# Cross-attention on one core: the third head group's last probability sum behind the fourth group's first maximum, and the hand-on of the largest weight moved into the third batch

## Chip, cores, metric

The kernel runs on one core of a Trainium2 chip. The metric is the time on the device in microseconds, of one execution. All times in this text are microseconds unless they are marked ns. The engines are TensorE (PE, and PEld for its weight loads), VectorE (DVE), ScalarE (ACT), GpSimd (POOL) and SyncE (SP, which issues most DMA transfers).

## What is computed

One block of a perceiver: x (8 batches of 128 rows of 512) attends to a context (8 batches of 2048 rows), then to itself with weights and activations quantised to 8 bits, then goes through a mixture of 8 experts. The change touches the first third and one number that the second needs, the largest absolute weight.

```python
def cross_attention(query, context, Wq, Wk, Wv, Wo):      # 16 heads of 32
    Q, K, V = query @ Wq.T, context @ Wk.T, context @ Wv.T
    scores = einsum('bqhd,bkhd->bhqk', Q, K) / sqrt(32)
    attn = softmax(scores, axis=-1)
    return einsum('bhqk,bkhd->bqhd', attn, V).reshape(B, 128, 512) @ Wo.T

def fake_quant(x):                                        # per tensor, 8 bits
    scale = maximum(max(abs(x)) / 127, 1e-8)
    return round(clip(x / scale, -128, 127)) * scale

x = x + cross_attention(layernorm(x), ctx_1024, ...)
x = x + self_attention_quantised(layernorm(x), fake_quant(in_w), fake_quant(out_w), ...)
x = x + experts(layernorm(x), ...)
```

## The kernel before

Everything around the change is `cross_attention`. It runs over 8 batches (b = 0 to 7) and in each over 4 head groups of 4 heads (g = 0 to 3); the order on each engine is written out by hand, in one `body(b, last)` for each engine, and the engines meet by semaphores. About 136 us go by per batch.

For each group TensorE first makes the scores of 128 queries and 2048 keys in four pieces of 512 keys (`scores_for_max`, L900), each for four heads at once into `sc`, all four banks of it. VectorE reads each piece and takes the maximum per row (`maximum`, L656); TensorE may write the next piece only when the maximum has read the last (semaphore `m_read`). Between the pieces TensorE works on projections of keys or values for later groups (L861, L875), so that it need not stand still. Then the maxima go through a diagonal matrix (`maxima_to_diag`, L660, L664) and one matmul into a row of the stacked queries `qs` (L915), and TensorE makes the scores a second time, transposed and less the maximum (`scores_transposed`, L935), in 8 units of 256 keys. For that the keys have to be stacked in `ks` (high and low halves, moved by 12 DMA transfers of SP's queue for each group, `stack_k`, L298), and the queries in `qs` (12 transfers for each batch, L288). ScalarE takes the exponential of each unit into `probs` (L489), which has room for four units. TensorE multiplies each with the values (`times_v`, L952).

The denominators of the softmax are the sums over keys. VectorE adds units 0, 1, 4, 5, 6 into `acc_v` in four instructions (`add_probs(b, g, part)`, part 0 at L675, parts 1 to 3 at L678); GpSimd adds units 2, 3 and 7 into `acc_g` (L383, L388), then `acc_v` to it (L391, which waits for all four of VectorE's parts by `sum_v`) and folds it (L393). TensorE turns that into denominators (`denominators`, L972) after the four score pieces of the group that follows.

VectorE also makes the low halves of the next group's keys (`split_k`, L616), which the key stack and a bank of `proj` wait for, and in the third and fourth group the low halves of the next batch's context (`split_ctx`, L610). In the fourth group's case the last part of the sums already stands behind the first maximum of the next batch; in the other three groups it stands before the next group's first maximum. In batch 0 VectorE also takes the maximum over pieces of the weights (`largest_weight`, L810).

The pieces of the weights come by GpSimd's queue (`load_weight`, L347): four in each group of batch 0. When VectorE has seen all 16 (batch 1, group 1), it sets `wmax_ready`. GpSimd hands the two partial maxima on between batch 1 and batch 2: out to DRAM in `wmax` (L418), a wait until they have landed, and back to all partitions in `wq_all`, which lies in `xn2` (L420). Behind that it loads the first two weight pieces again, for the quantisation in the last batch.

Of the kernel before, what the change touches and what calls it, by code (L numbers as in the profile page):

```python
# [14 lines left out]
P = 128  # L15
B, T, D = 8, 128, 512
# [89 lines left out]
def cross_attention(nc, x, ctxT, wqT, wkT, wvT, woT, wiT, qoT, in_b, weights_q, wmax, wscale, wide_stage, stage_in, shared, x1, x1_stats, ident, ident16, ones, ones16):  # L106
# [4 lines left out]
    with ExitStack() as c:  # L111
# [154 lines left out]
        with nc.Block() as block:  # L266
# [71 lines left out]
            def _(gp):  # L338
                gp.memset(ks[QK:P, :, :], 1.0).then_inc(rows_set, 1)

                def load_weight(n, round_trip):
# [4 lines left out]
                        gp.wait_ge(wq_seen, WPIECES)  # L346
                    gp.dma_start(wq_f[:, n % 2, :], weight_piece(n)).then_inc(wq_in[n % 2], 16)  # L347

                def quantise_weight(n):
                    which = n // (3 * EC)  # L350
                    gp.wait_ge(wq_in[n % 2], 16 * (WPIECES // 2 + n // 2 + 1))
                    gp.tensor_scalar(wq_f[:, n % 2, :], wq_f[:, n % 2, :], wq_inv[:, which:which + 1], ROUND,
                                     ALU.mult, ALU.add).then_inc(wq_int, 1)
                    gp.wait_ge(wq_int, 2 * n + 1)
                    if n >= 2:
                        gp.wait_ge(wq_out[n % 2], 16 * (n // 2))
                    gp.tensor_scalar(wq_i[:, n % 2, :], wq_f[:, n % 2, :], -ROUND, 1.0, ALU.add, ALU.mult).then_inc(wq_int, 1)
                    gp.wait_ge(wq_int, 2 * n + 2)
                    gp.dma_start(weights_q[:, n // EC, n % EC, :], wq_i[:, n % 2, :]).then_inc(wq_out[n % 2], 16)
                    if n + 2 < WPIECES:  # L360
                        load_weight(n + 2, 1)
# [9 lines left out]
                def body(b, last):  # L371
                    for g in range(G):
                        e = 32 * b + UNITS * g
                        if first_batch(b) and g:
                            load_weight(4 * g, 0)
                            load_weight(4 * g + 1, 0)

                        at = 16 * b + 4 * g
                        if not (last and g == 3):
                            gp.wait_ge(e_ready, e + 4)  # L380
                            if not (isinstance(b, int) and b == 0 and g == 0):
                                gp.wait_ge(group_done, 4 * b + g)
                            gp.tensor_tensor(acc_g[:, :], probs[:, 2, :], probs[:, 3, :], ALU.add).then_inc(sum_g, 1)  # L383
                            if first_batch(b):
                                load_weight(4 * g + 2, 0)
                            gp.wait_ge(e_ready, e + 8)
                            gp.wait_ge(sum_g, at + 1)
                            gp.tensor_tensor(acc_g[:, :], acc_g[:, :], probs[:, 3, :], ALU.add).then_inc(sum_g, 1)  # L388
                            gp.wait_ge(sum_v, at + 4)
                            gp.wait_ge(sum_g, at + 2)  # L390
                            gp.tensor_tensor(acc_g[:, :], acc_g[:, :], acc_v[:, :], ALU.add).then_inc(sum_g, 1)  # L391
                            gp.wait_ge(sum_g, at + 3)
                            gp.tensor_tensor(acc_g[:, 0:512], acc_g[:, 0:512], acc_g[:, 512:1024], ALU.add).then_inc(sum_g, 1)  # L393
                        if first_batch(b):
                            load_weight(4 * g + 3, 0)
                        if last:
                            for n in range(*((0, 6), (6, 11), (11, WPIECES), (WPIECES, WPIECES))[g]):
                                if n == 2 * EC:
                                    gp.wait_ge(rows_scaled, 1)
                                    normalise(0)  # L400
                                    normalise(1)
                                quantise_weight(n)
                            if g == 2:
                                normalise(2)
                                normalise(3)
# [7 lines left out]
                load_weight(1, 0)  # L413
                body(0, False)

                body(1, False)
                gp.wait_ge(wmax_ready, 1)
                gp.dma_start(wmax[:, :], wq_part[:, :]).then_inc(wmax_moved, 16)  # L418
                gp.wait_ge(wmax_moved, 16)
                gp.dma_start(wq_all[:, :, :], wmax.rearrange("(a p) w -> a p w", a=1).to_broadcast([P, P, 2])).then_inc(wmax_moved, 16)  # L420
                load_weight(0, 1)
                load_weight(1, 1)
                for b in range(2, B - 1):
                    body(b, False)
                gp.wait_ge(wq_scaled, 1)
                body(B - 1, True)
# [172 lines left out]
            def _(dve):  # L599
# [120 lines left out]
                def body(b, last, steps):  # L720

                    first = first_batch(b)
                    for g in range(G):
                        for kb in range(KB):
                            maximum(b, g, kb)
                            if g == 0 and kb == 0 and not first:
                                add_probs(b - 1, 3, 3)
                            if first and g == 1 and kb:
                                row_stats(range((1, 4, 6)[kb - 1], (4, 6, 8)[kb - 1]), steps)
                            if first and g == 2 and kb == 0:  # L730
# [50 lines left out]
                        for part in range(4):  # L781
                            if ahead and part == 1:
                                split_k(nb, ng, 1)
                                if g == 2 and not last:
                                    split_ctx(b + 1, 2)
                            if g < 3 or not last and part < 3:
                                add_probs(b, g, part)
                            if ahead and part > 1:
                                split_k(nb, ng, part)
# [1686 lines left out]
```

## Time and profile before

| | us |
|---|---|
| median of 3 runs | 1725.7 |
| lowest and highest | 1724.34, 1726.32 |
| span of the profiled execution | 1727.4 |

The page gives no time for the profiled execution but its span, so that is what a sum is made against.

| engine | busy us | share of the span |
|---|---|---|
| PE | 1628.6 | 94% |
| DVE | 1171.3 | 68% |
| ACT | 767.5 | 44% |
| POOL | 471.1 | 27% |

The cross-attention fills the span up to about 1126 us, the quantised self-attention to about 1265, and the experts the rest. TensorE is close to full throughout, so small holes in its timeline count and what other engines do beside it does not, as long as it doesn't wait for them. In a timeline an idle time before an instruction stands in brackets, with the engine and line that ended it.

### The profile page before, as it was taken

How to read it: one execution, taken by the hardware profiler on the slowest of the kernel's cores; microseconds unless marked ns; L12 is line 12 of the kernel's file. 1: busy time of each engine (PE TensorE's matmuls, PEld its weight loads, DVE VectorE, ACT ScalarE, POOL GpSimd, SP SyncE). 2: the span in 40 equal slices, each digit the busy share in tenths (PEclk: the TensorE clock that was granted, in tenths of full speed). 3: DMA queues.
4: the chain of work that ended last, by engine and by line, in shares of the span. 5: the costliest groups of instructions: out<-in, count | busy, mean ns of one | idle time of the engine just before them, and what ended most of it. 6: DMA issues, size and time to landing. Idle time of an engine off the chain costs nothing. (4 is left out here: it accounts for less than half of the span.)

```text
span 1727.4 us, 39816 instructions
## 1 busy us (share of the span) xinstructions
PE 1628.6 (94%) x17264; PEld 1111.9 (64%) x17264; DVE 1171.3 (68%) x1400; ACT 767.5 (44%) x973; POOL 471.1 (27%) x412
## 2 busy tenths in 40 slices
PE   6999999999999999999999999896669999999998
PEld 4666666666666766666666666674447777777775
DVE  5678567457657757656766757557787767666766
ACT  5354336344444444435434533545445444344441
POOL 2323322232123123212222237632025411101133
PEclk9999999999999999999999999997879999999999
DMA  6544243334234233242233225460048655555544
GB/s 246 124 110 111 60 116 87 62 88 122 47 87 110 60 87 87 52 111 72 67 82 95 74 59 138 121 232 2 2 138 263 214 188 180 196 174 186 180 129 121
DMA packets 102151, 202.04 MB, mean 117 GB/s; under 512 B 25739, under 2 KB 25739, under 8 KB 101850
## 3 DMA queue, kind: packets, MB, share of 16 engines
q1 hardware_dynamic: 91258, 169.49, 34.1%
q0 software_dynamic: 10720, 30.02, 6.3%
q8 instruction: 137, 2.24, 0.6%
q14 instruction: 36, 0.29, 0.1%
HBM read 127.36 MB, written 18.90 MB: 85 GB/s over the span
## 5 line engine op out<-in xcount | busy, mean ns | idle before, releaser
L656 DVE TENSOR_REDUCE mx<-sc 128x4 f32<-128x2048 f32 x128 | 293.2, 2290 | 67.0 <-PE sc L900 66.4
L861 PE MATMUL proj<-w_hi,ctx 128*128 128x256 f16 x2048 | 273.7, 278 | 12.8 <-ACT ctx L441 12.6
L489 ACT ACTIVATE stage_w<-sc 128x1024 f32<-128x1024 f32 x256 | 248.2, 1024 | 70.8 <-PE sc L935 70.2
L875 PE MATMUL proj<-ctx,w_hi 128*128 128x512 f16 x1024 | 253.6, 380 | 0.0
L861 PEld LDWEIGHTS proj<-w_hi,ctx 128*128 128x128 f16 x2048 | 193.0, 99 | 64.6 <-issue 40.4
L452 ACT ACTIVATE stage_w<-proj 128x512 f32<-128x512 f32 x128 | 76.4, 597 | 340.8 <-PE proj L861 340.8
L383 POOL TENSOR_TENSOR acc_g<-stage_w 128x1024 f32<-128x1024 f32 x31 | 74.0, 2389 | 477.0 <-ACT stage_w L489 476.9
L678 DVE TENSOR_TENSOR acc_v<-acc_v,stage_w 128x1024 f32<-128x1024 f32 x93 | 131.9, 1418 | 87.1 <-ACT stage_w L489 84.3
L616 DVE SCALAR_TENSOR_TENSOR k_lo<-proj,k_hi 128x512 f16<-128x512 f32 x128 | 88.0, 687 | 118.6 <-ACT k_hi L461 117.7
L1166 DVE SCALAR_TENSOR_TENSOR w_lo<-stage_w,w_hi 128x2048 f16<-128x2048 f32 x64 | 144.8, 2293 | 34.2 <-ACT w_hi L1160 34.2
L875 PEld LDWEIGHTS proj<-ctx,w_hi 128*128 128x128 f16 x1024 | 90.1, 98 | 116.5 <-issue 25.1
L861 PE MATMUL proj<-w_lo,ctx 128*128 128x256 f16 x1024 | 157.9, 278 | 1.2 <-DVE w_lo L604 1.2
L1994 ACT ACTIVATE hf<-ph 128x321 f32<-128x321 f32 x128 | 56.3, 440 | 213.4 <-PE ph L2277 195.8
L2293 PE MATMUL po<-h_hi,w_hi 128*128 128x321 f16 x496 | 149.2, 301 | 0.3 <-issue 0.3
L2293 PE MATMUL po<-h_lo,w_hi 128*128 128x321 f16 x496 | 149.3, 301 | 0.0
L2293 PE MATMUL po<-h_hi,w_lo 128*128 128x321 f16 x496 | 149.2, 301 | 0.0
L935 PEld LDWEIGHTS sc<-qs,stage_w 97*128 97x128 f16 x2048 | 126.7, 99 | 32.8 <-DMA stage_w<-k_hi 5.0
L935 PE MATMUL sc<-qs,stage_w 97*128 97x128 f16 x2048 | 138.4, 221 | 5.3 <-DMA stage_w<-k_hi 3.5
L952 PE MATMUL po<-stage_w 128*32 128x128 f32 x4096 | 139.4, 277 | 0.0
L875 PE MATMUL proj<-ctx,w_lo 128*128 128x512 f16 x512 | 131.8, 380 | 0.0
L461 ACT ACTIVATE k_hi<-proj 128x512 f16<-128x512 f32 x128 | 76.5, 597 | 108.9 <-PE proj L875 104.1
L388 POOL TENSOR_TENSOR acc_g<-acc_g,stage_w 128x1024 f32<-128x1024 f32 x31 | 80.7, 2604 | 152.0 <-ACT stage_w L489 152.0
(354 smaller groups left out, 2488.8 us busy)
## 6 DMA issues: line engine op xcount, KB each, us to landing
stage_w<-in_w SPq DMA_DIRECT2D x64, 1024.0 KB, 5.9
ctx_stage<-in_ctxT SPq DMA_DIRECT2D x64, 512.0 KB, 4.6
stage_w<-k_hi SPq DMA_DIRECT2D x256, 128.0 KB, 2.4
stage_w<-k_lo SPq DMA_DIRECT2D x128, 128.0 KB, 2.4
wq_f<-in_wiT POOLq DMA_DIRECT2D x24, 256.0 KB, 4.4
xg<-xbuf POOLq DMA_DIRECT2D x28, 176.0 KB, 4.4
obuf<-o_sb POOLq DMA_DIRECT2D x28, 176.0 KB, 3.5
xbuf<-final SPq DMA_DIRECT2D x17, 256.0 KB
```

The costliest lines, as they stand in the source:

```text
L388: gp.tensor_tensor(acc_g[:, :], acc_g[:, :], probs[:, 3, :], ALU.add).then_inc(sum_g, 1)
L461: act.activation(k_hi[:, 512 * kb:512 * kb + 512], proj[where % 2][:, :], ACT.Copy, scale=1.0 / WSCALE).then_inc(proj_act, 1)
L489: act.activation(probs[:, u % 4, :], unit_scores(u), ACT.Exp, scale=1.0 / sqrt(HD)).then_inc(e_ready, 1)
L616: dve.scalar_tensor_tensor(k_lo[part], proj[where % 2][:, :], 1.0 / WSCALE, k_hi[part], ALU.mult, ALU.subtract).then_inc(k_low, 1)
L656: dve.tensor_reduce(mx[:, :, kb], sc[:, :, :], AX.X, ALU.max).then_inc(m_read, 1)
L678: dve.tensor_tensor(acc_v[:, :], acc_v[:, :], probs[:, (0, 0, 1, 2)[part], :], ALU.add).then_inc(sum_v, 1)
L861: last = pe.matmul(out, x_part[:, kb, e, col:col + P], w_part[:, 2, e, wv], start=term == 0 and e == 0, stop=term == 2 and e == EC - 1)
L875: last = pe.matmul(proj[at % 2][:, :], w_part[:, 1, e, P * (g % G):P * (g % G) + P], x_part[:, kb, e, :], start=term == 0 and e == 0, stop ...
L935: last = pe.matmul(sc[:, 2 * (u % 2) + i, P * j:P * j + P], ks[0:QKM, j, P * ck:P * ck + P], qs[0:QKM, 4 * g + j, :], start=True, stop=True)
L952: last = pe.matmul(po[HD * j:HD * j + HD, 0:T], v_sb[:, g // 2, ck, at:at + HD], probs[:, u % 4, 512 * i + P * j:512 * i + P * j + P], sta ...
L1166: dve.scalar_tensor_tensor(w_lo[:, s % NSPLIT], stage[:, s], WSCALE, w_hi[:, s % NSPLIT], ALU.mult, ALU.subtract).then_inc(stage_lo, 1)
L2293: last = pe.matmul(po[i][:, 0:CAP], w_part[:, s % NSPLIT, f, P * i:P * i + P], h_part[:, at, :], start=q == 0 and f == 0 and n == 0, stop= ...
```

## The change

VectorE: part 3 of the sums of the third group (g = 2) is no longer issued at the end of that group but behind the first maximum of the fourth (g = 3), in all eight batches.

GpSimd: the hand-on of the two partial maxima (a wait, a DMA, a wait until it has landed, a DMA) moves from between batch 1 and batch 2 into the first group of batch 2, between GpSimd's first and second add. The two weight loads that stood behind it move to the same place in the second group of batch 2.

```diff
+                def hand_on_largest():
+                    gp.wait_ge(wmax_ready, 1)
+                    gp.dma_start(wmax[:, :], wq_part[:, :]).then_inc(wmax_moved, 16)
+                    gp.wait_ge(wmax_moved, 16)
+                    gp.dma_start(wq_all[:, :, :], wmax.rearrange("(a p) w -> a p w", a=1).to_broadcast([P, P, 2])).then_inc(wmax_moved, 16)
...
                             if first_batch(b):
                                 load_weight(4 * g + 2, 0)
+                            if b == 2 and g == 0:
+                                hand_on_largest()
+                            if b == 2 and g == 1:
+                                load_weight(0, 1)
+                                load_weight(1, 1)
                             gp.wait_ge(e_ready, e + 8)
...
-                body(1, False)
-                gp.wait_ge(wmax_ready, 1)
-                gp.dma_start(wmax[:, :], wq_part[:, :]).then_inc(wmax_moved, 16)
-                gp.wait_ge(wmax_moved, 16)
-                gp.dma_start(wq_all[:, :, :], wmax.rearrange("(a p) w -> a p w", a=1).to_broadcast([P, P, 2])).then_inc(wmax_moved, 16)
-                load_weight(0, 1)
-                load_weight(1, 1)
-                for b in range(2, B - 1):
+                for b in range(1, B - 1):
                     body(b, False)
...
                             if g == 0 and kb == 0 and not first:
                                 add_probs(b - 1, 3, 3)
+                            if g == 3 and kb == 0:
+                                add_probs(b, 2, 3)
...
-                            if g < 3 or not last and part < 3:
+                            if g < 2 or part < 3 and not (last and g == 3):
                                 add_probs(b, g, part)
```

What the change moves on VectorE, at the step from the third to the fourth group of batch 1. The add into `acc_v` is part 3 of the sums, `k_lo` is the key split, `mx<-sc` a maximum. Before:

```order
L616 SCALAR_TENSOR_TENSOR k_lo<-proj0,k_hi 128x512
L610 TENSOR_TENSOR ctx<-ctx_stage,ctx 128x1024
L678 TENSOR_TENSOR acc_v<-acc_v,stage_w 128x1024
L616 SCALAR_TENSOR_TENSOR k_lo<-proj1,k_hi 128x512
L656 TENSOR_REDUCE mx<-sc 128x4 x4
L660 TENSOR_REDUCE nm<-mx 128x4
```

And now, in the changed kernel, whose lines are numbered a little higher:

```order
L620 SCALAR_TENSOR_TENSOR k_lo<-proj0,k_hi 128x512
L614 TENSOR_TENSOR ctx<-ctx_stage,ctx 128x1024
L620 SCALAR_TENSOR_TENSOR k_lo<-proj1,k_hi 128x512
L660 TENSOR_REDUCE mx<-sc 128x4
L682 TENSOR_TENSOR acc_v<-acc_v,stage_w 128x1024
L660 TENSOR_REDUCE mx<-sc 128x4 x3
```

The add went from ahead of the last key split to behind the first of the four maxima.

On GpSimd, from the end of batch 1 to the second group of batch 2. The adds into `acc_g` are the sums of the probabilities. Before:

```order
L393 TENSOR_TENSOR acc_g<-acc_g 128x512
L418 DMA wmax<-wq_part 128x2
L420 DMA xn2<-wmax 128x256
L347 DMA wq_f<-in_wiT 128x512 x2
L383 TENSOR_TENSOR acc_g<-stage_w 128x1024
L388 TENSOR_TENSOR acc_g<-acc_g,stage_w 128x1024
L391 TENSOR_TENSOR acc_g<-acc_g,acc_v 128x1024
```

And now:

```order
L404 TENSOR_TENSOR acc_g<-acc_g 128x512
L389 TENSOR_TENSOR acc_g<-stage_w 128x1024
L351 DMA wmax<-wq_part 128x2
L353 DMA xn2<-wmax 128x256
L399 TENSOR_TENSOR acc_g<-acc_g,stage_w 128x1024
L402 TENSOR_TENSOR acc_g<-acc_g,acc_v 128x1024
L404 TENSOR_TENSOR acc_g<-acc_g 128x512
L389 TENSOR_TENSOR acc_g<-stage_w 128x1024
L347 DMA wq_f<-in_wiT 128x512 x2
L399 TENSOR_TENSOR acc_g<-acc_g,stage_w 128x1024
```

Two of the four DMAs went behind the first add of batch 2, the other two behind the first add of its second group.

## Rows read from the trace of the kernel before

**Rows 1.** The page, busy time, share and instructions of each engine
```profile
PE 1628.6 (94%) x17264; PEld 1111.9 (64%) x17264; DVE 1171.3 (68%) x1400; ACT 767.5 (44%) x973; POOL 471.1 (27%) x412
```
**Rows 2.** Who waited for whom: total us, times, longest
```profile
PE sc L900 <- DVE mx L656: 18.2, 18, 2.9
```
**Rows 3.** Timeline (start, length), TensorE, group 3's score pieces, batches 2 and 1
```profile
418.23 0.40 PE L900 MATMUL sc<-k_hi,q_hi 32*128 32x512 f16 x4
...
423.27 0.40 PE L900 MATMUL sc<-k_hi,q_hi 32*128 32x512 f16 x4 [1.91 <-DVE mx L656]
...
426.32 0.40 PE L900 MATMUL sc<-k_hi,q_hi 32*128 32x512 f16 x4
...
280.74 0.40 PE L900 MATMUL sc<-k_hi,q_hi 32*128 32x512 f16 x4 [1.92 <-DVE mx L656]
...
285.46 0.40 PE L900 MATMUL sc<-k_hi,q_hi 32*128 32x512 f16 x4
```
**Rows 4.** Stretches: busy by engine, then granted clock, DMA share, GB/s
```profile
280.00:286.00 6.00, 5.26 (x34) 3.40 (x35) 2.98 (x3) 0.84 (x2) 1.48 (x2) 0.72 0.92 206
334.00:341.40 7.40, 7.26 (x25) 3.96 (x26) 1.92 (x2) 2.54 (x3) 0.00 (x0) 0.59 0.01 2
```
**Rows 5.** Timeline, VectorE, last add and first maximum, batch 2
```profile
416.93 3.39 DVE L678 TENSOR_TENSOR acc_v<-acc_v,stage_w 128x1024 f32<-128x1024 f32 x1
...
420.85 2.27 DVE L656 TENSOR_REDUCE mx<-sc 128x4 f32<-128x2048 f32 x1
```
**Rows 6.** Timeline, GpSimd and ScalarE, the same place
```profile
416.17 3.07 POOL L388 TENSOR_TENSOR acc_g<-acc_g,stage_w 128x1024 f32<-128x1024 f32 x1 [4.44 <-ACT stage_w L489]
...
417.33 0.60 ACT L461 ACTIVATE k_hi<-proj 128x512 f16<-128x512 f32 x1 [1.23 <-PE proj L875]
```
**Rows 7.** Timeline, TensorE and VectorE, first group of batch 3
```profile
457.78 0.39 PE L900 MATMUL sc<-k_hi,q_hi 32*128 32x512 f16 x4
...
460.95 0.40 PE L900 MATMUL sc<-k_hi,q_hi 32*128 32x512 f16 x4
...
457.38 1.22 DVE L678 TENSOR_TENSOR acc_v<-acc_v,stage_w 128x1024 f32<-128x1024 f32 x1
```
**Rows 8.** Timeline, TensorE, fourth group of batch 0
```profile
144.32 0.40 PE L900 MATMUL sc<-k_hi,q_hi 32*128 32x512 f16 x4 [2.95 <-DVE mx L656]
```
**Rows 9.** Timeline, TensorE and VectorE, fourth group of batch 7
```profile
1098.58 1.91 PE L92 MATMUL proj<-ctx_stage,wi_q 128*128 128x256 f16 x16 [1.62 <-issue]
...
1107.04 2.29 DVE L656 TENSOR_REDUCE mx<-sc 128x4 f32<-128x2048 f32 x1 [0.59 <-PE sc L900]
```
**Rows 10.** Timeline and DMA list (last: us to landing), hand-on and what follows
```profile
321.45 0.56 POOL L418 DMA_DIRECT2D wmax<-wq_part  x1
...
325.36 0.55 POOL L420 DMA_DIRECT2D xn<-wmax  x1 [3.36 <-DMA wmax<-wq_part]
...
wq_f<-in_wiT POOLq DMA_DIRECT2D x2, 256.0 KB, 7.2
...
334.14 1.89 PE L935 MATMUL sc<-qs,stage_w 97*128 97x128 f16 x16 [3.55 <-DMA stage_w<-k_hi]
...
335.82 5.74 PE L1021 MATMUL misc<-wo_sb,ot 128*128 128x512 f32 x8
...
343.12 1.06 PE L935 MATMUL sc<-qs,stage_w 97*128 97x128 f16 x16
...
472.18 3.65 PE L1021 MATMUL misc<-wo_sb,ot 128*128 128x512 f32 x8
```
**Rows 11.** Timeline, GpSimd, TensorE and SP's queue, the new places in batch 2
```profile
353.27 2.48 POOL L388 TENSOR_TENSOR acc_g<-acc_g,stage_w 128x1024 f32<-128x1024 f32 x1 [5.03 <-ACT stage_w L489]
...
377.22 2.37 POOL L383 TENSOR_TENSOR acc_g<-stage_w 128x1024 f32<-128x1024 f32 x1 [17.63 <-ACT stage_w L489]
...
367.66 0.43 PE L972 MATMUL po<-acc_g,ones 128*32 128x128 f32 x8
...
387.32 2.42 SPq L298 DMA_DIRECT2D stage_w<-k_hi  x4
```

## Prediction

> **What bounds the kernel now.** I read the page first, for the engine that fills the span: TensorE is busy for 94% of it, VectorE for 68%, so time can be won only where TensorE stands still or runs slowly [rows 1]. Next the list of who waited for whom, for TensorE inside the cross-attention: its reading of scores L900 waited 18.2 us in all, 18 times, for VectorE's maxima L656 [rows 2]. Then TensorE's timeline at those places. Three things are to be seen.
>
> First, the same wait stands at the same place in every batch but the last: between the first and the second score group of the fourth head group. The score groups of the third batch start at 418.23, 423.27 and 426.32 [rows 3]. The undisturbed distance is 426.32 - 423.27 = 3.05; the disturbed one is 5.04, so this place costs 1.99. I count six such rows (batches 1 to 6, counting from 0), distances 5.03 to 5.08; batch 0 waits 2.95 [rows 8]; batch 7 has another form of it.
>
> Second, in some batches the wait is followed by slow matmuls. In batch 1 the next distance is 285.46 - 280.74 = 4.72 instead of 3.05 with no wait in it [rows 3], and the granted clock of the stretch around it is 0.72, so part of it ran at 1.2 instead of 2.4 GHz [rows 4]. That is 1.67 more. Of the six, four show it (batches 1, 3, 4, 6), two don't although they waited as long (batch 2 in [rows 3] and batch 5), and batch 0 shows it too. What TensorE had done before was the same wait each time; so this part is not the same in each execution.
>
> Third, once, at the first score product of batch 2, TensorE waits 3.55 for the key stack to land, and then runs slowly: granted clock 0.59 [rows 4], 1.89 for sixteen matmuls that take 1.06 a little later, and 5.74 for the output projection that takes 3.65 one batch on [rows 10].
>
> **Part one: the third group's last add goes behind the fourth group's first maximum.** Why VectorE is late: its last add of the third group takes 3.39 [rows 5], where the same instruction takes 1.22 when GpSimd is idle [rows 7]. GpSimd's add L388 had begun 0.76 earlier, at 416.17, and ended at 419.24 [rows 6]; 3.39 is nearly the rest of that (2.31) and one undisturbed add (1.22). Behind it stand the key split and then the maximum, which starts at 420.85 although its scores were there at 418.63 [rows 3, 5]. The Trainium skill (SBUF — State Buffer, section "SBUF: two separate sides") states that a VectorE instruction with two SBUF inputs and a GpSimd one take a shared port pair in turn, each for its whole length. The row agrees, 3.39 against 2.31 + 1.22; the sum below goes by the rows alone.
>
> After the change the order is key split, first maximum, add, three maxima. The key copy that the split waits for ends at 417.93 [rows 6]. Before, the split filled the time between the add's end at 420.32 and the maximum at 420.85 [rows 5], so it needs 0.5 to 0.7; VectorE is free at 418.6 at the latest and the first maximum runs 418.7 to 421.0, its 2.27 [rows 5]. TensorE wants its second score group at 418.23 + 3.05 = 421.28: no wait is left. The add then runs 421.0 to 422.2. GpSimd's L388 is over by 419.3, and its next instruction waits for this very add, so nothing collides. What is late next is the second maximum, behind the add. The same order already stands one place further, where the fourth group's last add goes behind the next batch's first maximum: there the add takes 1.22 and the second-to-third distance is 460.95 - 457.78 = 3.17, against 3.05 [rows 7]. So the new cost is 0.11 a batch; the worst row of that kind (batch 7's first group) has 0.36 and 0.21 of wait, so 0.6 is the upper bound, and zero the lower. I take 0.11, of which there are five rows in batches 2 to 6.
>
> - Batches 1 to 6: 5.04 - 3.05 = 1.99 each (2.03 in one), six times 12.0, less 6 x 0.11 = 0.7: 11.3 gained.
> - The slow matmuls of batches 1, 3, 4, 6: about 1.66 each, 6.6 gained. Bounds: zero if something else brings them back, 6.6 if a wait of about 0.1 never does; none of the seven places of that kind, in front of batches 1 to 7, has a slow stretch behind it, so I take 6.6.
> - Batch 0: VectorE takes maxima over weight pieces there as well, and is later still. Its last add isn't held up there, so only the 1.2 of an undisturbed add leaves the queue ahead of the maximum. The maximum ends about 1.1 earlier, TensorE still waits 1.8 instead of 2.95 [rows 8], and the add pushes the second maximum back by 0.3: net 0.8. The slow stretch after it I leave as it is; if it goes too, 1.7 more.
> - Batch 7: the product behind the first scores waited 1.62 for the last key split, which stood behind the long add [rows 9]. It starts 1.6 earlier, but here VectorE is the slower one (maxima 2.29 plus 0.59 of hand-over), and gets the add (1.2) between its maxima. By my reckoning the last maximum starts at 1106.1 instead of 1107.04 [rows 9]: 0.9 gained. Bounds 0 and 1.6.
>
> GpSimd's last two adds of the third group wait for the moved add, so they start about 1.8 later, and TensorE asks for them 1.9 earlier. In the first group of batch 2 the add L388 ends at 355.75, two more of under 4 us together follow, and TensorE asks at 367.66 [rows 11]: 8 of cover. It shrinks to 4 and still hides them; without it TensorE's denominators would wait for the whole excess.
>
> **Part two: the largest weight is handed on inside batch 2.** Before, GpSimd's queue issued four DMAs at 321.4 to 327: the partial maxima out (1 KB), their copy to all partitions (128 KB), and two weight pieces of 256 KB, which took 7.2 to land [rows 10]. SP's 24 transfers of the query and key stacks run at the same time, and TensorE waits for the last of these at 334.14. In the other batches the stack lands without a wait. Cost: 3.55 waiting, 1.89 - 1.06 = 0.83 and 5.74 - 3.65 = 2.09 at the low clock [rows 10]: 6.5. All of it goes if the new places are quiet.
>
> The first two DMAs now stand between GpSimd's first and second add of batch 2's first group. GpSimd had 5.03 idle there [rows 11]; what comes in is 0.56 + 3.36 + 0.55 = 4.5 [rows 10]. It fits with 0.5 to spare; if it doesn't, the second add and its followers slip, with 8 us of cover before TensorE asks [rows 11]. The two pieces go out in the next group, behind its first add, which ends at 377.22 + 2.37 = 379.6, and SP's next key stack starts at 387.32 [rows 11]: 7.7 later, a little more than the 7.2 that they took in a crowd. So I take no new wait; the upper bound is the old one, 6.5.
>
> [...]
>
> **Sum.** 11.3 + 6.6 + 0.8 + 0.9 + 6.5 = 26.1 against the profiled execution's span of 1727.4. The median of the runs is 1725.7, 1.7 less, about one slow stretch of 1.67; if its run had one fewer, 24.4 is left to gain there. So 1699.6 to 1701.3; I say **1700.5**. Everything behind the cross-attention runs in TensorE's order and only starts earlier.
>
> **Rivals.**
> - A, the forecast: both waits go. 1699 to 1702, chance 0.76.
> - B, the slow stretches stay or appear elsewhere, since their cause is not the wait. For it: two equal waits without them. Against: no slow stretch in batches 1 to 6 without a wait before it. Gives up to 1700.5 + 6.6 + 2.9 (the hand-on's 0.83 + 2.09) = 1710, halfway 1705. Chance 0.09.
> - C, the hand-on's traffic makes a new wait where it now stands (the weight pieces against a key stack, or the copy to all partitions against context loads). For it: it did so once, with the same sizes. Against: 7.7 us of distance. Gives 1700.5 + 6.5 = 1707. Chance 0.09. [...]
> - D, slower: the moved add meets a GpSimd add and takes 3.39 again, now between the first and the second maximum. The third score group then waits 3.39 - 1.22 + 0.11 = 2.3 in each of eight batches, and each wait brings its slow stretch of 1.67: 8 x 3.95 = 31.6, and 1.8 are left in batch 0, 33.4 in all. The place costs now 12.0 + 6.6 + 4.6 (batch 0) + 1.6 (batch 7) = 24.8. So 8.6 more, less 6.5 for the hand-on: 1728; with C on top 1734. It decides if GpSimd's L388 is still running at 421.0, that is 1.8 later than it ends now. Against: it waits only for an exponential that doesn't move. Chance 0.03.
> - E, the waits are hidden behind something that the trace doesn't show and the time stays within 0.2%. Chance 0.03.
>
> **Chances.** A measurement of this kernel can tell about 0.2%, 3.5 us. Faster by more: A, B and C, 0.94; within: E and half of D, 0.04; slower: the rest, 0.02. The range 1697 to 1708: below, batch 0's slow stretch gone too and 2 us of scatter; above, C and most of B.
>
> **What would show it.** Right: score groups of the fourth head group 3.05, 3.17, 3.05 apart in batches 1 to 6; the moved add at 1.2; the maximum starting within 0.1 of its scores; no wait on the key stack in batch 2 and granted clock 1.00 there; batch 0 still waiting nearly 2 us. Wrong, if the moved add takes over 2 us (D), a wait on the key stack shows at another group of batch 2 (C), or distances of 4.7 appear without a wait before them (B).

## Result and the profile after

The changed kernel takes 1701.99 us (median of 4 runs, 1701.73 to 1705.24) against 1725.02 us for the kernel before (median of 4, 1721.54 to 1726.32): ratio 0.9871, 95% interval 0.9855 to 0.9887. The prediction was 1700.5, range 1697 to 1708. The span of the profiled execution went from 1727.4 to 1699.8, by 27.6 where the sum said 26.1. Two executions that stood far outside the rest, one of run e10 (2108.85) and one of the kernel before beside it (5763.49), are left out of the times below.

Two terms are used throughout. A distance is the time from the start of one score piece on TensorE to the start of the next, 3.05 when nothing disturbs it. A slow stretch is one in which the granted clock falls to its lower level, 1.2 instead of 2.4 GHz; in most cases it makes a distance of about 4.7 out of 3.05.

The page of the changed kernel, the line of busy times that answers to [rows 1]; no instruction came or went, and TensorE is busy for 11.2 us less, which is about what five slow stretches of 1.67 and the 2.9 behind the hand-on's wait come to (11.3):

```profile
PE 1617.4 (95%) x17264; PEld 1106.4 (65%) x17264; DVE 1156.8 (68%) x1400; ACT 767.6 (45%) x973; POOL 471.5 (28%) x412
```

Who waited for whom in the changed kernel (total, times, longest), the answer to [rows 2]. 18.2 us of waiting for maxima became 5.6, of which the longest, 1.8, is batch 0's:

```profile
PE sc L906 <- DVE mx L660: 5.6, 13, 1.8
```

The timeline of the changed kernel at the fourth group of batch 2 (start, length; TensorE, then VectorE, then GpSimd), the answer to [rows 3, 5, 6]:

```profile
405.40 0.40 PE L906 MATMUL sc<-k_hi,q_hi 32*128 32x512 f16 x4
...
408.45 0.39 PE L906 MATMUL sc<-k_hi,q_hi 32*128 32x512 f16 x4
...
411.61 0.40 PE L906 MATMUL sc<-k_hi,q_hi 32*128 32x512 f16 x4
...
405.12 0.69 DVE L620 SCALAR_TENSOR_TENSOR k_lo<-proj,k_hi 128x512 f16<-128x512 f32 x1 [0.92 <-ACT k_hi L465]
405.84 2.29 DVE L660 TENSOR_REDUCE mx<-sc 128x4 f32<-128x2048 f32 x1
408.05 1.22 DVE L682 TENSOR_TENSOR acc_v<-acc_v,stage_w 128x1024 f32<-128x1024 f32 x1
...
403.34 3.09 POOL L399 TENSOR_TENSOR acc_g<-acc_g,stage_w 128x1024 f32<-128x1024 f32 x1 [4.42 <-ACT stage_w L493]
...
409.35 2.35 POOL L402 TENSOR_TENSOR acc_g<-acc_g,acc_v 128x1024 f32<-128x1024 f32 x1 [2.92 <-DVE acc_v L682]
```

Score groups 3.05 and 3.16 apart, the add at 1.22 instead of 3.39, the maximum 0.04 behind its scores. GpSimd's add ended at 406.43, well ahead of VectorE's at 408.05, and its next one starts when that ends. VectorE now even waits 0.92 ahead of the key split, where it had been the late one.

Batch 0 (TensorE), the answer to [rows 8], and two stretches of the changed kernel (busy time by engine, then granted clock), the answer to [rows 4]:

```profile
138.05 0.40 PE L906 MATMUL sc<-k_hi,q_hi 32*128 32x512 f16 x4
...
142.97 0.40 PE L906 MATMUL sc<-k_hi,q_hi 32*128 32x512 f16 x4 [1.80 <-DVE mx L660]
...
146.31 0.40 PE L906 MATMUL sc<-k_hi,q_hi 32*128 32x512 f16 x4 [0.21 <-DVE mx L660]
...
142.00:148.00 6.00, 4.82 (x45) 3.75 (x46) 5.41 (x4) 2.29 (x3) 3.89 (x3) 1.00 1.06 222
324.00:331.00 7.00, 7.00 (x47) 3.92 (x46) 2.61 (x3) 2.56 (x5) 0.00 (x0) 1.00 0.01 2
```

The wait is down to the 1.8 forecast, but nothing slow follows it: granted clock 1.00 (first stretch). The second stretch is the beginning of batch 2's transposed scores, where the clock had been 0.59.

The hand-on in its new places (GpSimd, with the list's median of 3.0 from issue to landing, then SP's queue) and TensorE at the old wait, the answer to [rows 10, 11]:

```profile
335.34 0.56 POOL L351 DMA_DIRECT2D wmax<-wq_part  x1
339.09 0.55 POOL L353 DMA_DIRECT2D xn<-wmax  x1 [3.19 <-DMA wmax<-wq_part]
340.44 2.48 POOL L399 TENSOR_TENSOR acc_g<-acc_g,stage_w 128x1024 f32<-128x1024 f32 x1 [0.80 <-ACT stage_w L493]
...
366.74 1.08 POOL L347 DMA_DIRECT2D wq_f<-in_wiT  x2
...
wq_f<-in_wiT POOLq DMA_DIRECT2D x2, 256.0 KB, 3.0
...
374.48 2.42 SPq L298 DMA_DIRECT2D stage_w<-k_hi  x4
...
324.18 1.06 PE L941 MATMUL sc<-qs,stage_w 97*128 97x128 f16 x16
...
325.07 3.65 PE L1027 MATMUL misc<-wo_sb,ot 128*128 128x512 f32 x8
```

The hand-on fits into GpSimd's idle time with 0.80 to spare (forecast 0.5), and the pieces are issued 7.7 ahead of the next key stack. Both groups of matmuls run at full clock, at once.

Where the 27.6 us came from, by the starts of the output projection (L1021 before, L1027 after), one in each batch. The last row goes from that of batch 6, issued in batch 7, to the self-attention's first product on `ot` (1128.83 and 1101.22):

| stretch, from its first to its last | before | after | less |
|---|---|---|---|
| start to batch 0's (in batch 1) | 195.37 | 192.66 | 2.71 |
| to the next (fourth group of batch 1, slow stretch, hand-on wait) | 140.45 | 132.41 | 8.04 |
| (slow projection, fourth group of batch 2) | 136.36 | 132.41 | 3.95 |
| (fourth group of batch 3, slow stretch) | 135.99 | 132.40 | 3.59 |
| (batch 4, slow stretch) | 135.89 | 132.41 | 3.48 |
| (batch 5) | 134.28 | 132.41 | 1.87 |
| (batch 6, slow stretch) | 136.53 | 132.99 | 3.54 |
| (batch 7) | 113.96 | 113.53 | 0.43 |

The sum is 27.6: all of it lies in the cross-attention. Behind it the two profiled executions are alike within 0.1 (598.6 and 598.6 to the end).

### The profile page after: what moved, and what is told of

Read it like the earlier page. It is cut to its first block and busy times, and to the rows that moved or that the text cites. A ratio compares the mean times of both kernels' runs of the same rounds, so it can differ in the third digit from the quotient of the medians.

```text
span 1699.8 us, 39816 instructions
## 1 busy us (share of the span) xinstructions
PE 1617.4 (95%) x17264; PEld 1106.4 (65%) x17264; DVE 1156.8 (68%) x1400; ACT 767.6 (45%) x973; POOL 471.5 (28%) x412
## 5 line engine op out<-in xcount | busy, mean ns | idle before, releaser
L867 PE MATMUL proj<-w_hi,ctx 128*128 128x256 f16 x2048 | 268.6, 274 | 12.6 <-ACT ctx L445 12.5
L682 DVE TENSOR_TENSOR acc_v<-acc_v,stage_w 128x1024 f32<-128x1024 f32 x93 | 116.1, 1248 | 87.2 <-ACT stage_w L493 84.4
L867 PE MATMUL proj<-w_lo,ctx 128*128 128x256 f16 x1024 | 154.3, 273 | 1.2 <-DVE w_lo L608 1.2
L941 PE MATMUL sc<-qs,stage_w 97*128 97x128 f16 x2048 | 137.6, 220 | 1.8 <-ACT stage_w L493 1.0
```

Source lines behind the costliest of these rows:

```text
L682: dve.tensor_tensor(acc_v[:, :], acc_v[:, :], probs[:, (0, 0, 1, 2)[part], :], ALU.add).then_inc(sum_v, 1)
L867: last = pe.matmul(out, x_part[:, kb, e, col:col + P], w_part[:, 2, e, wv], start=term == 0 and e == 0, stop=term == 2 and e == EC - 1)
L941: last = pe.matmul(sc[:, 2 * (u % 2) + i, P * j:P * j + P], ks[0:QKM, j, P * ck:P * ck + P], qs[0:QKM, 4 * g + j, :], start=True, stop=True)
```

## Experiments

All kernels were compared with runs of the kernel before on their own chip. Since executions of one kernel spread by 3 to 9 us here, the verdicts on single places rest on distances in the traces, and the times are given beside them.

### Each half of the change alone

```diff
 # e1_add_alone: the kernel before, and
+                            if g == 3 and kb == 0:
+                                add_probs(b, 2, 3)
...
-                            if g < 3 or not last and part < 3:
+                            if g < 2 or part < 3 and not (last and g == 3):
```

> VectorE's part alone: the third group's last add behind the fourth group's first maximum; the hand-on stays between batch 1 and 2. Theory (the two parts are separate and add up): the score distances of the fourth group are 3.05, 3.16, 3.05 in batches 1 to 6, no slow stretch there, and batch 2 keeps its wait of about 3.5 on the key stack with a low clock behind it; 6.5 us over the changed kernel, so 1708.5. Rival (slow stretches have a cause of their own and come back elsewhere): 1710 to 1718, with distances of 4.7 that have no wait ahead. Rival (the hand-on's wait came from TensorE's late arrival and goes with the first part): 1702.

Measured: 1705.51 (1703.16 to 1707.16) against 1725.88, ratio 0.9885 (0.9862 to 0.9907). The distances of the fourth group are 3.05, 3.16 or 3.17, 3.05 in batches 1 to 6, with no slow stretch. The wait on the key stack is there, a little shorter. TensorE in batch 2 of this kernel:

```profile
328.64 1.89 PE L937 MATMUL sc<-qs,stage_w 97*128 97x128 f16 x16 [2.46 <-DMA stage_w<-k_hi]
```

So the wait doesn't come from TensorE's late arrival, and 2.46 of 3.55 remain of it. From projection to projection the two batches are 135.81 and 133.21 against 132.41 in the changed kernel: 4.2 us, not 6.5. The rest (wait, matmuls at the low clock) follows as before.

```diff
 # e2_handon_alone: the changed kernel, and
-                            if g == 3 and kb == 0:
-                                add_probs(b, 2, 3)
...
-                            if g < 2 or part < 3 and not (last and g == 3):
+                            if g < 3 or not last and part < 3:
```

> GpSimd's part alone: the hand-on and the two weight pieces inside batch 2, VectorE's order as before. Theory: no wait on the key stack in batch 2, clock 1.00 there; the waits of 1.92 in batches 1 to 6 and 2.95 in batch 0 stay, three to seven of them with a slow stretch of 1.67 behind. 6.5 us under the kernel before: 1718.5. Rival (the stack's wait only moves): no change, 1725.

Measured: 1722.17 (ten runs, 1719.73 to 1727.72) against 1725.88, ratio 0.9983 (0.9966 to 0.9999). No wait on the key stack. The waits of about 1.93 are all there, and slow stretches follow in batches 3, 5 and 6, not in 0, 1, 2 and 4. TensorE of this kernel, batches 2 and 3, and two stretches behind the waits (the number that is 1.00 and 0.72 is the granted clock):

```profile
413.62 0.40 PE L904 MATMUL sc<-k_hi,q_hi 32*128 32x512 f16 x4 [1.94 <-DVE mx L660]
...
547.92 0.40 PE L904 MATMUL sc<-k_hi,q_hi 32*128 32x512 f16 x4 [1.93 <-DVE mx L660]
...
552.64 0.40 PE L904 MATMUL sc<-k_hi,q_hi 32*128 32x512 f16 x4
...
413.00:419.00 6.00, 5.38 (x51) 4.28 (x52) 4.64 (x3) 1.80 (x3) 1.36 (x2) 1.00 0.92 206
547.90:553.90 6.00, 5.98 (x41) 4.19 (x42) 3.11 (x2) 1.16 (x2) 0.84 (x1) 0.72 0.89 199
```

Two equal waits, one with and one without the low clock behind it, and in other batches than in the kernel before. So the length of the wait alone doesn't decide whether a slow stretch of 1.67 follows; what does stays open, and how many an execution gets differs from one to the next. The halves add up: 20.4 and 3.7 make 24.1, against 23.0 for both together, within the spread (the interval of the second half alone goes from 0.2 to 5.9).

### Why VectorE was late: GpSimd's add, not too much work

```diff
 # e3_short_gpsimd_add: the kernel before, and
-                            gp.tensor_tensor(acc_g[:, :], acc_g[:, :], probs[:, 3, :], ALU.add).then_inc(sum_g, 1)
+                            cols = 1 if g == 2 else 1024
+                            gp.tensor_tensor(acc_g[:, 0:cols], acc_g[:, 0:cols], probs[:, 3, 0:cols], ALU.add).then_inc(sum_g, 1)
```

> The kernel before, with GpSimd's second add of the third group (L388) cut from 1024 columns to one; the denominators of that group then lack most of one unit. Nothing is moved. Theory (VectorE is late because its add is held by GpSimd's, not because it has too much to do): the add takes 1.2 instead of 3.39, the first-to-second score distance of the fourth group falls from 5.04 to 3.05 to 3.2 in batches 1 to 6, and in batch 0, where the context split beside GpSimd's add shrinks from 2.5 to 1.2, from 6.07 to about 4.8; no slow stretches. Time as in the run with VectorE's part alone, 1707 to 1709. Rival (too much work ahead of the first maximum, whatever GpSimd does): distances stay at 5.0, time 1725.

Measured: 1706.64 (1704.46 to 1710.21), ratio 0.9897 (0.9871 to 0.9922). VectorE, GpSimd and TensorE of this kernel at the fourth group of batch 2, in the old order:

```profile
409.58 1.22 DVE L679 TENSOR_TENSOR acc_v<-acc_v,stage_w 128x1024 f32<-128x1024 f32 x1
...
411.31 2.28 DVE L657 TENSOR_REDUCE mx<-sc 128x4 f32<-128x2048 f32 x1
...
408.78 0.93 POOL L389 TENSOR_TENSOR acc_g<-acc_g,stage_w 128x1 f32<-128x1 f32 x1 [4.40 <-ACT stage_w L490]
...
410.84 0.40 PE L901 MATMUL sc<-k_hi,q_hi 32*128 32x512 f16 x4
...
413.90 0.40 PE L901 MATMUL sc<-k_hi,q_hi 32*128 32x512 f16 x4
```

With GpSimd's add all but gone and nothing moved, VectorE's add takes 1.22 and the distance is 3.06. In batch 0 the distance is 4.78 as expected, and the context split 1.21 instead of 2.51. So the whole wait of the batches 1 to 6 was the collision, and VectorE's queue was otherwise just in time. The change doesn't lighten VectorE; it moves the add out of the stretch in which GpSimd has its own. (The wait on the key stack, 2.77, remains in this kernel.)

### What brings the slow matmuls

```diff
 # e6_maximum_twice: the changed kernel, and
                 def maximum(b, g, kb):
                     dve.wait_ge(m_ready, 16 * b + 4 * g + kb + 1)
+                    if g == 3 and kb == 0:
+                        dve.tensor_reduce(mx_extra[:, :], sc[:, :, :], AX.X, ALU.max)
```

> The changed kernel, with the first maximum of the fourth group taken twice in each batch (2.29 more on VectorE, from PSUM; the first result is thrown away). It brings back a wait of about 2.0 ahead of the second score group and about 0.4 ahead of the third, without the old order and without a collision. Theory (a wait of this size is what brings the slow stretches): 8 x 2.5 = 20, and 4 to 8 slow stretches of 1.67: 1728 to 1735. Rival (the slow stretches belong to the old order or to the collision): waits, but no slow stretch: 1722.

Measured: 1730.00 (ten runs, 1724.76 to 1733.66), ratio 1.0026 (1.0011 to 1.0040). The wait is 1.96 in batches 1 to 6 and 4.01 and 2.66 in batches 0 and 7. The next distance is about 4.7 in batches 0, 1, 3, 4, 5 and not in 2, 6, 7. TensorE in batches 1 and 2:

```profile
282.60 0.40 PE L909 MATMUL sc<-k_hi,q_hi 32*128 32x512 f16 x4 [1.96 <-DVE mx L663]
...
287.32 0.39 PE L909 MATMUL sc<-k_hi,q_hi 32*128 32x512 f16 x4
...
418.58 0.40 PE L909 MATMUL sc<-k_hi,q_hi 32*128 32x512 f16 x4 [1.96 <-DVE mx L663]
...
421.91 0.40 PE L909 MATMUL sc<-k_hi,q_hi 32*128 32x512 f16 x4 [0.21 <-DVE mx L663]
```

4.72 in one batch, 3.33 in the other. Neither the old order nor the collision is needed: the wait alone brings them, sometimes. The rival is out.

Batch 7 has a slow stretch too, though its distance of 3.33 hides it. The matmuls behind its wait of 2.66 take 2.90, where the same sixteen take 1.92 in run e7 below. The time is not lost, because in e7 the third piece waits 1.08 there for ScalarE and here it doesn't. TensorE of this kernel, then of e7:

```profile
1098.35 0.40 PE L909 MATMUL sc<-k_hi,q_hi 32*128 32x512 f16 x4 [2.66 <-DVE mx L663]
1098.68 2.90 PE L92 MATMUL proj<-ctx_stage,wi_q 128*128 128x256 f16 x16
```
```profile
1083.06 1.92 PE L92 MATMUL proj<-ctx_stage,wi_q 128*128 128x256 f16 x16
```

```diff
 # e7_maximum_half_more: the changed kernel, and
+                    if g == 3 and kb == 0:
+                        dve.tensor_reduce(mx_extra[:, 0:2], sc[:, 0:2, :], AX.X, ALU.max)
```

> The changed kernel, with half of the first maximum of the fourth group taken once more (about 1.2 on VectorE, result thrown away). Theory: a wait of about 0.9 ahead of the second score group and 0.4 ahead of the third, 8 x 1.3 = 10, and no slow stretches behind waits this short, since those of 0.4 to 1.8 in the changed kernel had none: 1712. Rival (any wait of about 1 is enough to bring them): 1719 to 1725.

Measured: 1713.12 (1710.62 to 1716.37), ratio 0.9929 (0.9909 to 0.9948). The waits are 0.89 (batches 1 to 6) and 1.59 (batch 7), without a slow stretch; batch 0 waits 2.94 and has one. TensorE in batch 1:

```profile
279.57 0.40 PE L909 MATMUL sc<-k_hi,q_hi 32*128 32x512 f16 x4 [0.89 <-DVE mx L663]
...
282.90 0.40 PE L909 MATMUL sc<-k_hi,q_hi 32*128 32x512 f16 x4 [0.21 <-DVE mx L663]
```

Over these four traces (before, e2, e6, e7): of 23 waits of 1.9 to 4.0 at this place, 15 have a slow stretch behind them (5 of 7, 3 of 7, 6 of 8, 1 of 1), and 14 of the 15 lengthened the next distance. Of the shorter ones none has: seven of 0.9 to 1.6 in e7, and the one of 1.2 to 1.8 in batch 0 of the changed kernel and of nine runs below and above (e1, e3, e4, e5, e8 to e12).

### Which of the hand-on's DMAs delayed the key stack

The first two put one half of the traffic back between batches 1 and 2.

```diff
 # e4_pieces_at_old_place: the changed kernel, and
-                            if b == 2 and g == 1:
-                                load_weight(0, 1)
-                                load_weight(1, 1)
...
-                for b in range(1, B - 1):
+                body(1, False)
+                load_weight(0, 1)
+                load_weight(1, 1)
+                for b in range(2, B - 1):
```

> The changed kernel, with the two weight pieces (2 x 256 KB) loaded again between batch 1 and 2, while the hand-on (1 KB out, 128 KB to all partitions) stays in batch 2. Theory (what delays the key stack is the bytes that run beside it): the pieces are 512 of 640 KB, so most of the wait comes back: 1.5 to 3.5 on the key stack, 3 to 6 us with the slow matmuls, 1705 to 1708. Rival (it is the copy to all partitions or the late time at which it is issued): no wait, 1702.

```diff
 # e5_handon_at_old_place: the changed kernel, and
-                            if b == 2 and g == 0:
-                                hand_on_largest()
...
-                for b in range(1, B - 1):
+                body(1, False)
+                hand_on_largest()
+                for b in range(2, B - 1):
```

> The changed kernel, with the hand-on (1 KB out, wait, 128 KB to all partitions) between batch 1 and 2 again, and the two weight pieces in batch 2's second group. Theory (bytes beside the key stack): 128 KB are as much as one of the stack's 12 transfers, so no wait or under 0.5, 1702 to 1702.5. Rival (the copy to all partitions is what delays it): the wait of 3.5 and its slow stretch are back, 1708.5.

Measured: 1704.93 (1702.53 to 1706.96) and 1705.06 (1704.36 to 1705.42). The wait on the key stack is 0.55 with the pieces and 0.17 with the hand-on. So the first expectation was wrong: 512 of the 640 KB bring back a sixth of the wait, and the two halves together, 0.7, are far from 2.46 to 3.55. What differed was the time: in the kernel before the pieces go out only after the 1 KB has landed, at 325.9, beside the last four of the key stack's transfers; alone they go out 4 us earlier, measured back from the moment at which TensorE wants the stack. Two more runs were made on that.

```diff
 # e9_pieces_late: the changed kernel, without the first three lines of hand_on_largest and
 # without the two load_weight in batch 2, and between batches 1 and 2
+                gp.wait_ge(wmax_ready, 1)
+                gp.dma_start(wmax[:, :], wq_part[:, :]).then_inc(wmax_moved, 16)
+                gp.wait_ge(wmax_moved, 16)
+                load_weight(0, 1)
+                load_weight(1, 1)
 # the copy to all partitions stays in batch 2, group 0
```

> The changed kernel, with the 1 KB transfer, the wait for it and then the two weight pieces between batch 1 and 2, so that these are issued some 4 to 5 us later than in the run with the pieces alone at the old place (0.55 of wait there); the 128 KB copy to all partitions stays in batch 2. Theory (what counts is that bytes are issued beside the last of the key stack's transfers): the wait on the key stack is 1.5 to 2.5, with slow matmuls behind it if it is near 2. Rival (all 640 KB must come together for it): 0.6 or less.

```diff
 # e10_all_pieces_first: the changed kernel, without the hand-on and the two load_weight in batch 2,
 # and between batches 1 and 2
+                load_weight(0, 1)
+                load_weight(1, 1)
+                hand_on_largest()
```

> The changed kernel, with all four of the moved DMAs between batch 1 and 2 again, but the two weight pieces ahead of the 1 KB transfer, so that they are issued 4 to 5 us earlier than in the kernel before. Theory (time of issue): 0.5 to 1.0 of wait on the key stack, the 0.55 of the pieces and the 0.17 of the copy together, no slow matmuls. Rival (sum of bytes): 2.5 to 3.5 as with VectorE's part alone and in the kernel before.

Measured: 1704.71 (1703.36 to 1705.65), ratio 0.9866 (0.9839 to 0.9893), and 1701.99 (three runs, 1701.29 to 1705.57), ratio 0.9863 (0.9825 to 0.9901). TensorE in batch 2 of the four kernels, in the order e4, e5, e9, e10:

```profile
325.68 1.07 PE L941 MATMUL sc<-qs,stage_w 97*128 97x128 f16 x16 [0.55 <-DMA stage_w<-k_hi]
```
```profile
324.93 1.07 PE L941 MATMUL sc<-qs,stage_w 97*128 97x128 f16 x16 [0.17 <-DMA stage_w<-k_hi]
```
```profile
325.86 1.07 PE L941 MATMUL sc<-qs,stage_w 97*128 97x128 f16 x16 [0.83 <-DMA stage_w<-k_hi]
```
```profile
324.58 1.07 PE L940 MATMUL sc<-qs,stage_w 97*128 97x128 f16 x16 [0.40 <-DMA stage_w<-k_hi]
```

| issued between the batches | pieces issued, us before TensorE wanted the stack | wait |
|---|---|---|
| 1 KB, copy (e5) | not there | 0.17 |
| pieces, 1 KB, copy (e10) | 9.1 | 0.40 |
| pieces (e4) | 9.1 | 0.55 |
| 1 KB, pieces (e9) | 5.2 | 0.83 |
| 1 KB, copy, pieces (e1) | 5.2 | 2.46 |
| the same (e3) | 5.1 | 2.77 |
| the same, kernel before | 4.7 | 3.55 |

Neither theory holds alone. That the late time alone does it is out by e9 (0.83 where it said 1.5 to 2.5). That the bytes count as a sum, whenever they are issued, is out by e4 and e10 (0.55 and 0.40 where it said at least 1.5 and 2.5). But e10 doesn't put all 640 KB beside the stack: its 1 KB took 5.86 behind the pieces, so the copy went out at 322.52, only 1.7 before TensorE wanted the stack. A run with all the bytes at the late time, but the pieces ahead of the copy, would tell more and wasn't made. What is shown is that only the copy and both pieces issued back to back, beside the end of the key stack, made a wait of over 1 us, in three kernels of three. What they share there, and why it is 3.55 in one kernel and 2.46 in another, stays open.

The four small waits can't be ranked. A wait of that size also comes and goes one batch earlier, at the first score product of batch 1, where none of the moved transfers is issued: it is absent from the first profile of the changed kernel and 0.54 in a second one (e12, below), 0.55 in e1 and 0.28 to 0.31 in e3, e8 and e9. TensorE of e12:

```profile
192.48 1.07 PE L941 MATMUL sc<-qs,stage_w 97*128 97x128 f16 x16 [0.54 <-DMA stage_w<-k_hi]
```

For the use it doesn't matter: loading the pieces ahead of the hand-on (e10, 1701.99) gave as much as moving both did (1701.99), as far as the times can tell.

### Two attempts at a better kernel

```diff
 # e8_weight_maxima_later: the changed kernel, and
+                            if first and g == 3 and kb in (1, 2):
+                                largest_weight(8 + kb)
...
-                            if first and g + part:
+                            if first and g + part and not (g == 2 and part > 1):
                                 largest_weight(4 * g + part - 1)
```

> The changed kernel, with two of batch 0's maxima over weight pieces (0.67 each) moved from ahead of the fourth group's first score maximum to behind its second and third. Theory: the wait of 1.80 in batch 0 falls by 1.2 to 1.3, to about 0.5: 1700.7. It may be eaten in part by GpSimd's next piece loads, which wait for these maxima, if a later maximum then waits for its piece. Rival (they hide something that comes next, the context split held by GpSimd's add): less than 0.4 gained.

Measured: 1703.27 (1701.64 to 1705.68), ratio 0.9868 (0.9851 to 0.9886): no gain to be told. In batch 0 the wait fell from 1.80 to 1.21, half of what was expected, and in batch 7 a wait of 1.09 came where there had been 0.41. Both have one cause. VectorE and GpSimd in this kernel, batch 0 and then batch 7:

```profile
136.08 3.08 DVE L614 TENSOR_TENSOR ctx<-ctx_stage,ctx 128x1024 f16<-128x1024 f32 x1
...
135.72 2.36 POOL L399 TENSOR_TENSOR acc_g<-acc_g,stage_w 128x1024 f32<-128x1024 f32 x1 [0.46 <-ACT stage_w L493]
...
1034.72 3.23 DVE L682 TENSOR_TENSOR acc_v<-acc_v,stage_w 128x1024 f32<-128x1024 f32 x1
...
1034.50 2.36 POOL L399 TENSOR_TENSOR acc_g<-acc_g,stage_w 128x1024 f32<-128x1024 f32 x1 [2.72 <-ACT stage_w L493]
```

The context split starts 0.6 earlier but stands behind the same GpSimd add and ends at the same distance from it: 3.08 instead of 2.48. Taking work away ahead of an instruction that is held gives nothing until the hold ends. In batch 7 GpSimd's add came 0.22 ahead of VectorE's this time; in the changed kernel VectorE's came 0.86 ahead and took 1.22. Nothing orders the two, so a shift of 1 us somewhere earlier decides about 2 us here.

```diff
 # e11_last_batch: the changed kernel, and
-                            if g == 3 and kb == 0:
-                                add_probs(b, 2, 3)
+                            if (g == 3 or last and g == 2) and kb == 0:
+                                add_probs(b, g - 1, 3)
...
-                            if last and g == 2 and kb == 0:
+                            if last and g == 2 and kb == 1:
...
-                            if g < 2 or part < 3 and not (last and g == 3):
+                            if part < 3 and not (last and g == 3) or part == 3 and (g == 0 or g == 1 and not last):
```

> The changed kernel, with the second group's last add also behind the third group's first maximum in the last batch, and that batch's variances behind the second maximum instead of the first. Theory: the wait of 0.41 at the third group's third score piece of batch 7 falls to 0.1, and VectorE's last add there cannot be held by GpSimd's, as it was in the run with the weight maxima moved (3.23, wait 1.09). 0.3 to 0.5 us, far less than the times can tell: 1702. Rival: the small variance instruction waits for GpSimd's adds at its new place too and nothing is gained.

Measured: 1703.84 (1703.49 to 1706.51), ratio 0.9863 (0.9836 to 0.9890). The distances of batch 7's third group are 3.06, 3.16, 3.78, and VectorE's add took 1.21 there: the wait of 0.41 at the third piece went, and one of 0.66 came at the fourth. The small variance instruction took 1.07 at its new place, beside GpSimd's add, so the rival was right. Neither attempt beats the changed kernel.

### The changed kernel once more

> The changed kernel once more, to see how far its time and the length of its stages move by themselves. Theory: the cross-attention is as long as in its first profile within 0.5 (but for slow stretches), and what moves is in the self-attention behind it, by 1 to 3; median 1702 to 1705. Rival: the runs with a DMA back at its old place were slower by their waits alone, and this one is at 1702.0 within 0.5.

Measured: 1702.00 (1700.20 to 1702.86), ratio 0.9851 (0.9823 to 0.9879). The distances of the fourth group are those of its first profile to 0.01 or 0.02, the stretch up to batch 0's output projection is 0.7 longer (with the 0.54 shown above), batch 7 is 0.6 shorter, and the self-attention is as long (from its product on `ot` to the router's first transpose 135.8 both times). So the result repeats within less than I expected. That stretch took 137.6 in e4, 137.5 in e5 and e9, 137.3 in e8 and 137.8 in e11, and 135.8 in e10, although its code is the same. What comes behind it differs as well: 464.0 to 464.6 in the same five, 462.5 to 462.8 in e10 and in both profiles of the changed kernel. These five are the ones whose medians lie 1.3 to 3.1 over 1702.0, so that excess is for the most part there, not in the waits of 0.2 to 0.8. What moves it stays open.

## Why the prediction was right

- **The fourth group's wait in batches 1 to 6** (forecast 12.0 less 0.7): measured 1.88 a batch, 11.3. The new distance was 3.16 or 3.17, as in the place that it was read from. The cause, the collision with GpSimd's add, is shown by e3.
- **The slow stretches** (forecast 6.6): gone from batches 1, 3, 4, 6. That they hang on the wait is shown by e6 and e7; that a wait gets one only sometimes, by e2 and e6. The 6.6 is therefore the count of the one profiled execution: with as many waits e2 had three, not four, in these six batches.
- **Batch 0** (forecast 0.8, and 1.7 more if its slow stretch goes too): the two distances went from 6.07 and 4.72 to 4.92 and 3.34, so 2.5 less together. The wait was sized rightly, 1.80; to leave the slow stretch in was wrong. This is most of the 1.5 by which the span's gain was over the sum.
- **Batch 7** (forecast 0.9): its fourth group gained 0.92, but a wait of 0.41 came in its third, for which I had no term. A variance of 128x7 numbers took 0.99 there instead of 0.29; it ends with GpSimd's add. VectorE and GpSimd of the changed kernel:

```profile
1040.38 0.99 DVE L757 TENSOR_SCALAR var<-mv 128x7 f32<-128x7 f32 x1
...
1040.08 1.27 POOL L404 TENSOR_TENSOR acc_g<-acc_g 128x512 f32<-128x512 f32 x1
```

- **The hand-on** (forecast 6.5): in the profiled executions 6.6 (8.04 + 3.95, less twice 1.88 and one slow stretch of 1.66). Against the kernel before, e2 gives 3.7, and e1, which keeps it, is 3.5 over the changed kernel. Its wait is 2.46, 2.77 and 3.55 in three kernels that have it, so 6.5 is the upper end of what it costs.
- **From the span to the median** was the step that was off, and in two ways that nearly cancel. I read the median, 1.7 under the span, as one slow stretch fewer. But the time is not the span: the changed kernel's profiled execution took 1701.77 with a span of 1699.8, so some 2.0 lie around it, and the profiled execution of before, with 5 slow stretches and the longest of the three waits on the stack, took 1729.29, some 4 over its median. Against the median the gain is 23.0, not 24.4 to 26.1. So the doubt that mattered was in the starting point, and my range had no term for it. That the time still came out within 1.5 of the forecast is in part luck: the sum read the gains of an execution with more to lose than most, and batch 0's slow stretch, which it left in, went as well.
- **Rival B** (slow stretches of another cause) is refuted by e6 and e7, **C** (the traffic waits elsewhere) by the trace after: a distance of 7.7 to the next key stack, landing in 3.0 instead of 7.2. **D** (a collision at the new place) didn't occur: in batch 2 GpSimd's add was over 1.6 before the moved add started. A collision of that kind at another place is what e8 met in batch 7: where nothing orders the two engines, it can come.

## What to carry to other kernels

Where two engines' elementwise instructions on SBUF run at the same time, look at their lengths next to the undisturbed ones before counting work: here one add held 2.2 us at the wrong place cost TensorE 2 us in each of six batches, and placing it behind a maximum that reads PSUM cost 0.11. Price a short wait of TensorE with what follows it: waits of 1.9 to 4.0 us had slow matmuls behind them in 15 of 23 cases, which cost about 1.67 us in 14, and waits up to 1.8 never had at this place. And take the gain against the median, not the profiled execution, if the two differ in how many such events they caught.

## What was not expected of the hardware

- A tiny VectorE instruction is held to the end of GpSimd's add just as a large one is: 128x7 numbers took 0.99 and 1.07 beside such adds instead of 0.29.
- Waits of the same length at the same place (1.93 and 1.94, e2) had the low clock behind them in one batch and not in the other.
- DMA traffic of two queues did not add up: waits of 0.17 and 0.55 on the key stack for the parts, 2.46 to 3.55 for both back to back.
